# Experts and attention: statistics in two batches with powers on GpSimd, weight remainders spread over the steps, one-hot rows column by column

## The chip, the cores and the metric

The kernel runs on one core of one Trainium2 chip, as one launch. The metric is the device time in microseconds (us). The median of the three timed runs before the change is 2083.06 us.

## What is computed

`x` is (4, 1024, 256) in fp32, that is 4096 tokens of 256 numbers. Four layers follow one another; each normalises its input by rows and adds its result to `x`:

```python
x = x + attn_a(layernorm(x))     # a recurrent memory over chunks of 64 tokens
x = x + ffn(layernorm(x))        # 8 experts, 2 per token, and a shared one
x = x + attn_b(layernorm(x))     # softmax attention, 16 heads of 16
x = x + ffn(layernorm(x))

def layernorm(x):  return (x - mean(x)) / sqrt(var(x) + 1e-5)
def ffn(x):        # I = 352
    probs = softmax(x @ gate_w.T);  w, i = top_k(probs, 2);  w = w / w.sum()
    combine = sum(one_hot(i, 8) * w)
    out = sum_e combine[e] * ((silu(x @ w_gate[e]) * (x @ w_up[e])) @ w_down[e])
    return out + sigmoid(x @ shared_gate_w) * ((silu(x @ sw_gate) * (x @ sw_up)) @ sw_down)
```

Attention runs over four sequences of 1024 tokens.

## The kernel before

The residual X stays in on-chip memory as 32 tiles of 128 rows by 256. The kernel is a sequence of phases with a barrier between them: memory (`attn_a`), experts (`ffn_phase`, tag moe1), query/key/value projection (`qkv_phase`), scores, output projection, experts again (moe2). Within a phase each engine has its own instruction stream, written out by hand, and the streams meet at semaphores; so the order in each stream is the order of the work. Each phase that adds to X also leaves `stats` (bn_stats) of its rows for the next phase's normalisation.

**Opening of an expert phase.** VectorE (L404 to L415) aggregates the statistics of all 32 tiles into `mv` (L408, `var_done`), waits for `w_high`, subtracts the high part of the shared expert's weights (L412, one 128x1428 operation, `w_rest`), waits for `std_done` and takes the reciprocal of the root (L414). ScalarE (L308 to L314) loads the Sqrt table, copies the router's columns, casts the shared weights to their high part (L311), takes the root (L313) and loads the Silu table. Then VectorE normalises tile 0 (L431) and TensorE, which has waited, transposes it (L719).

**Precision.** Weights and rows are each split into a high part (fp32r) and a remainder; gate and up are three products (L794, L795, L799). The high parts of the 8 experts' weights are cast in 16 pieces of 128x704 by ScalarE (`weights_high`, L319) and the remainders subtracted by VectorE (`weights_rest`, L423), in place: `W_rest` lies where `W_gate_up` lay. The first 20 steps use the shared expert alone, so the experts' remainders are needed from step 20 on.

**Steps.** Step n handles one tile of 128 rows: transposition (L719), gate and up, silu (ScalarE, L341) times up (VectorE, `hidden`, L600), transposition of that (L809), down (L824), and the addition to X (`add_shared`, L604). `source_rest` (L427) subtracts the remainder of the transposed rows. The first four steps (LOOK = 4) are "looking" steps: beside its own tile each transposes 7 more (BESIDE = 7) and computes their router logits (`extra`, `extras`, L736), so that after step 3 all 32 tiles have logits. VectorE's own step n issues `hidden` for step n + 1 and `source_rest` for n + 2; in the looking steps it ends with `weights_rest`: 2, 4, 5 and 5 pieces. In step 4 `choose_first` copies the logits out of their bank (L459, `lg_ready`), for which down(4) waits; steps 4 to 7 choose the experts, count and compute positions.

**One-hot pieces.** In steps 8 to 15 (`one_hots(i)`, 8 columns each) VectorE compares broadcasts into `hot_j` (L552, 128x576) and `hot_p` (L554, 128x1024) and multiplies (L557, 128x576), all bf16, with drains between; ScalarE scales `hot_j` by the lane (`lanes`, L349). TensorE multiplies the pieces (`inverse`, L753) into a table of which token goes to which slot. After that come the routed blocks, fetched and sent by GpSimd's indirect DMAs (L269, L278).

**Attention.** `qkv_phase` opens as the experts do, without weights: Sqrt table, 8 memsets, 32 aggregations, root, reciprocal, then four tiles at a time (CT = 4) are normalised (`rows`, L1746), transposed (L1786) and projected (L1806). `out_projection_phase` opens with four copies by ScalarE (L2122) that TensorE transposes (L2148).

**GpSimd** builds constants at the start of an expert phase (L245 to L258), then waits for the slots. In the memory phase it takes one square root per chunk as a power (L1028).

## Time and profile before

| | us |
|---|---|
| median of three timed runs | 2083.06 |
| the three runs | 2081.0, 2083.06, 2090.43 |
| the profiled execution | 2093.06 |
| its span, first to last instruction | 2091.3 |

| engine | busy us | share of the span |
|---|---|---|
| TensorE (matmuls) | 1950.0 | 93% |
| VectorE | 1273.1 | 61% |
| ScalarE | 1136.9 | 54% |
| GpSimd | 424.3 | 20% |

The phases in the profiled execution, by the start of their first instructions: experts from 272.0 us, attention's projection from 733.7, output projection from about 1584.3, experts again from 1625.0. The mean granted TensorE clock is 0.965 of full.

How to read it: a line number is that of the kernel before. PE is TensorE's matmuls, PEld its weight loads, DVE is VectorE, ACT ScalarE, POOL GpSimd, SPq the queue that issues DMAs. A timeline row merges neighbouring instructions of one kind: its second number runs from the start of the first to the end of the last. In square brackets stands how long the engine was idle before the row and what released it. PEclk is the granted clock as a part of 2.4 GHz.

### The profile page before, as it was taken

To read this page: it belongs to the slowest core of one execution; us is meant where nothing else is said; L and a number is where in the kernel's file an instruction comes from. 1 tells how busy PE (TensorE), PEld (TensorE's weight loads), DVE (VectorE), ACT (ScalarE), POOL (GpSimd) and SP (SyncE) were. 2 spreads that over 40 slices of the span, in tenths; PEclk is the share of its full clock that TensorE was granted. 3 is DMA by queue.
4 is the path that set the end of the run, shared out by engine and by line. 5 is a ranking of instruction groups with operands and counts; after the bars stand their busy time and mean duration, and the time that the engine had idled before them with its cause. 6 is when DMAs were issued, how large, how long until landed. Compare 5 with 4: busy or idle time off the path is not lost. (4 is left out here: it accounts for less than half of the span.)

```text
span 2091.3 us, 52175 instructions
## 1 busy us (share of the span) xinstructions
PE 1950.0 (93%) x19334; PEld 1476.0 (71%) x19335; DVE 1273.1 (61%) x2596; ACT 1136.9 (54%) x2301; POOL 424.3 (20%) x495
## 2 busy tenths in 40 slices
PE   6899888999999879899999999999998889999997
PEld 6577677899999743355556555565546778999996
DVE  6455457622222857699999999999935585222226
ACT  2311153344444243389889899898995533444442
POOL 1021100255544132200000000000000002555542
PEclk9999969999999989999999999999999799999999
DMA  7000021122222456332111221111004211222226
GB/s 282 0 1 0 0 91 29 35 70 71 71 70 72 178 151 173 104 87 53 39 39 39 53 54 44 38 39 38 3 3 192 91 31 34 71 70 70 70 73 258
DMA packets 85433, 151.03 MB, mean 72 GB/s; under 512 B 35844, under 2 KB 67844, under 8 KB 78916
## 3 DMA queue, kind: packets, MB, share of 16 engines
q1 hardware_dynamic: 71620, 110.09, 17.3%
q0 software_dynamic: 13632, 38.41, 6.0%
q8 instruction: 129, 2.11, 0.4%
q14 instruction: 52, 0.43, 0.1%
HBM read 99.30 MB, written 48.76 MB: 71 GB/s over the span
## 5 line engine op out<-in xcount | busy, mean ns | idle before, releaser
L1932 ACT ACTIVATE att_scores_pt<-att_scores_psE 128x512 f32<-128x512 f32 x1024 | 598.1, 597 | 68.3 <-PE att_scores_psE L1535 26.0
L1550 DVE TENSOR_REDUCE att_mx<-att_scores_psS 128x1 f32<-128x1024 f32 x472 | 578.1, 1225 | 49.5 <-PE att_scores_psS L1535 18.1
L1535 PE MATMUL att_scores_psE<-att_qs,att_ks 99*32 99x512 bf16 x4096 | 438.0, 382 | 6.2 <-DVE att_scores_psO L1962 5.5
L2034 PE MATMUL att_scores_psO<-att_scores_pt,att_va 128*17 128x256 f32 x4096 | 330.5, 379 | 2.9 <-ACT att_scores_osb L1937 1.3
L824 PE MATMUL moe_ps<-W_down,work 128*128 (+1 forms) x1236 | 309.6, 387 | 13.9 <-DVEq L460 6.5
L1535 PE MATMUL att_scores_psS<-att_ks,att_qs 96*32 96x512 bf16 x3776 | 308.8, 380 | 0.1
L795 PE MATMUL moe_ps<-W_rest,moe_srcT_high 128*128 (+2 forms) x824 | 271.5, 330 | 0.0
L591 DVE SCALAR_TENSOR_TENSOR moe_pick<-work,moe_pick 128x2 f32 (+1 forms) x142 | 22.8, 161 | 407.9 <-PE moe_ps L799 407.9
L824 PEld LDWEIGHTS moe_ps<-W_down,work 128*128 128x128 f32 x1236 | 221.6, 192 | 42.8 <-issue 19.1
L1535 PEld LDWEIGHTS att_scores_psE<-att_qs,att_ks 99*32 99x32 bf16 x4096 | 136.8, 95 | 105.3 <-ACT att_scores_pt L1932 8.7
L2034 PEld LDWEIGHTS att_scores_psO<-att_scores_pt,att_va 128*17 128x17 f32 x4096 | 132.1, 98 | 102.4 <-issue 12.9
L794 PE MATMUL moe_ps<-moe_gate_up_high,moe_srcT_high 128*128 x568 | 196.5, 346 | 0.0
L269 POOL DMA_INDIRECT work<-normalised_rows,moe_slots_i x142 | 138.0, 972 | 287.3 <-DVE moe_slots_i L577 244.7
L278 POOL DMA_INDIRECT expert_rows<-work,moe_slots_i x142 | 140.2, 987 | 248.3 <-ACT work L356 236.7
L1535 PEld LDWEIGHTS att_scores_psS<-att_ks,att_qs 96*32 96x32 bf16 x3776 | 126.8, 98 | 77.3 <-issue 1.3
L337 ACT CAST moe_srcT_high<-moe_ps 128x256 fp32r<-128x256 f32 x206 | 76.6, 372 | 166.2 <-PE moe_ps L719 166.2
L795 PEld LDWEIGHTS moe_ps<-W_rest,moe_srcT_high 128*128 128x128 f32 x824 | 159.8, 194 | 0.0
L345 ACT COPY work<-moe_ps 128x384 f32<-128x384 f32 x206 | 97.8, 475 | 110.8 <-PE moe_ps L809 110.8
L356 ACT ACTIVATE work<-moe_ps,moe_y_weight 128x256 f32<-128x256 f32 x142 | 67.3, 474 | 154.6 <-PE moe_ps L824 154.6
L341 ACT ACTIVATE moe_hid<-moe_ps 128x352 f32<-128x352 f32 x206 | 95.4, 463 | 81.1 <-PE moe_ps L799 81.1
L799 PE MATMUL moe_ps<-moe_gate_up_high,moe_srcT_rest 128*128 x568 | 138.1, 324 | 0.0
L600 DVE TENSOR_TENSOR moe_hid<-moe_hid,moe_ps 128x352 f32<-128x352 f32 x206 | 106.6, 518 | 41.4 <-PE moe_ps L799 38.4
(286 smaller groups left out, 2739.3 us busy)
## 6 DMA issues: line engine op xcount, KB each, us to landing
work<-expert_rows SPq DMA_DIRECT2D x16, 1024.0 KB, 6.6
W_gate_up<-in_gate_up_dram SPq DMA_DIRECT2D x2, 6346.0 KB, 21.9
query_key_parts<-att_qkv_parts SPq DMA_DIRECT2D x64, 192.0 KB, 2.8
normalised_rows<-work SPq DMA_DIRECT2D x64, 128.0 KB, 1.8
work<-normalised_rows SPq DMA_DIRECT2D x56, 128.0 KB, 2.2
att_qs<-query_key_parts SPq DMA_DIRECT2D x16, 384.0 KB, 4.3
att_ks<-query_key_parts SPq DMA_DIRECT2D x16, 384.0 KB, 4.4
W_down<-in_down_a_dram SPq DMA_DIRECT2D x2, 2304.0 KB, 27.3
```

The source lines that it names most:

```text
L269: nc.gpsimd.indirect_dma_start(out=src[u][:, :], out_offset=None, in_=xn_d, in_offset=bass.IndirectOffsetOnAxis(ap=slots_i[:, j, 0:1].bitc ...
L278: nc.gpsimd.indirect_dma_start(out=ys, out_offset=bass.IndirectOffsetOnAxis(ap=slots_i[:, j, 1:2].bitcast(U32), axis=0), in_=yb[j % 2][:, ...
L345: nc.scalar.copy(hidT[u][:, :, :].rearrange("p k t -> p (k t)"), psH[:, 0:IP]).then_inc(hidT_ready, 1)
L600: nc.vector.tensor_tensor(hid[u][:, 0:I], hid[u][:, 0:I], psU[u][:, 0:I], ALU.mult).then_inc(hid_ready, 1)
L794: nc.tensor.matmul(psum, srcT_high[u][:, k, :], high(k), start=(k == 0), stop=False)
L795: nc.tensor.matmul(psum, srcT_high[u][:, k, :], rest(k), start=False, stop=False)
L799: last = nc.tensor.matmul(psum, srcT_rest[u][:, k, :], high(k), start=False, stop=(k == KD - 1))
L824: last = nc.tensor.matmul(psD[:, 0:D], hidT[u][:, k, :], W["down"][:, k, e, :], start=(k == 0), stop=(k == KI - 1))
L1535: last = nc.tensor.matmul(out[j:j + 32, :], stationary[:, j:j + 32], moving, start=True, stop=True, tile_position=(0, j), skip_group_check ...
L1550: return nc.vector.tensor_reduce(a.mx[g % 2][:, v:v + 1], bank[:, :, :].rearrange("p h k -> p (h k)"), AX.X, ALU.max)
L1932: nc.scalar.activation(pt[s % 2][:, r, :], psE[use % E_BANKS][:, :], ACT.Exp, scale=HD ** -0.5).then_inc(p_ready, 1)
L2034: last = nc.tensor.matmul(psO[32 * r:32 * r + VC, cols], va[g][:, kt, r * VC:(r + 1) * VC], pt[s % 2][:, r, cols], start=(kt == 0 and part ...
```

## The change

In the expert phases:

- The statistics are aggregated in two batches, the first 11 tiles (FIRST = LOOK + BESIDE) and the other 21. VectorE adds eps into `spread`, and GpSimd raises it to the power -0.5 into `rstd`. Root, reciprocal and both table loads go.
- ScalarE copies router columns and casts the shared weights in two halves; VectorE subtracts them in two halves (`shared_rest`), one ahead of the wait for the first powers, one between extra(1) and source_rest(0).
- The second batch of statistics, and the wait for its powers, stand behind the extras of step 0 and ahead of those of step 1.
- GpSimd casts the first four of the experts' 16 weight pieces, ScalarE the other twelve, in looking steps 0 to 2. The remainders are subtracted in steps 0, 1, 2 (4, 4 and 8 pieces), in two portions around `hidden`, instead of 2, 4, 5, 5 at the ends of steps 0 to 3.
- The one-hot rows are written by 3 x 8 tensor-scalar operations per piece, of 128, 72 and 72 columns, each against a pointer to a column of `pos_p` or `pos_j` (now fp32). `hot_j`, `tile1` and ScalarE's `lanes` go.

In `qkv_phase` the same split of the statistics (4 and 28 tiles) with powers on GpSimd; the memsets of `vt` move behind the second batch. In `out_projection_phase` ScalarE loads the Silu table first.

The diff, cut to its core:

```diff
@@ -183,6 +181,11 @@
+        def weights_high(nc, copy, i):
...
+            e, k = divmod(i, KD)
+            return copy(H[:, k, e * GU:(e + 1) * GU], W["gate_up"][:, k, e * GU:(e + 1) * GU])
@@ -242,6 +245,13 @@
         def _(pool):
+            nc.gpsimd.memset(minus_half[:, :], -0.5).then_inc(half_set, 1)
+            pool.wait_ge(half_set, 1)
+            for i, some in enumerate((slice(0, FIRST), slice(FIRST, NT))):
+                pool.wait_ge(var_done, i + 1)
+                nc.gpsimd.tensor_tensor(rstd[:, some], spread[:, some], minus_half[:, some], ALU.pow).then_inc(rstd_ready, 1)
+            for i in range(KD * E // LOOK):
+                weights_high(nc, nc.gpsimd.tensor_copy, i).then_inc(w_high, 1)
@@ -305,18 +314,10 @@
         def _(act):
-            nc.scalar.preload_act_table(ACT.Sqrt)
...
-            nc.scalar.copy(router[:, :, :], W["gate_up"][:, :, (E + 1) * GU:])
-            nc.scalar.copy(W["shared_high"][:, :, :], W["gate_up"][:, :, E * GU:]).then_inc(w_high, 1)
-            act.wait_ge(var_done, 1)
-            nc.scalar.activation(rstd[:, :], mv[:, :, 1], ACT.Sqrt, bias=eps[:, :]).then_inc(std_done, 1)
-            nc.scalar.preload_act_table(ACT.Silu)
...
-            def weights_high(i):
...
-                e, k = divmod(i, KD)
-                nc.scalar.copy(H[:, k, e * GU:(e + 1) * GU], W["gate_up"][:, k, e * GU:(e + 1) * GU]).then_inc(w_high, 1)
+            for k in range(KD):
+                nc.scalar.copy(router[:, k, :], W["gate_up"][:, k, (E + 1) * GU:])
+                nc.scalar.copy(W["shared_high"][:, k, :], W["gate_up"][:, k, E * GU:]).then_inc(shared_high, 1)
             def extra_out(x):
@@ -369,15 +366,13 @@
-                if 0 <= here - LOOK - 6 < CH // PIECE:
-                    lanes(here - LOOK - 6)
...
-                        if i < 2 + KD * E // LOOK:
-                            weights_high(n * (KD * E // LOOK) + i - 2)
+                        if n + 1 < LOOK and i < 2 + KD * E // LOOK:
+                            weights_high(nc, nc.scalar.copy, (n + 1) * (KD * E // LOOK) + i - 2).then_inc(a_high, 1)
@@ -401,25 +396,27 @@
         def _(dve):
-            nc.vector.memset(eps[:, :], EPS)
-            for u in range(2):
-                nc.vector.memset(hid[u][:, I:IP], 0.0)
-            for t in range(NT):
-                nc.vector.bn_aggr(mv[:, t, :], stats[:, t, :])
-            dve.drain().then_inc(var_done, 1)
-            dve.wait_ge(w_high, 1)
-            raw = W["gate_up"][:, :, E * GU:]
-            nc.vector.tensor_tensor(W["rest"][:, :, E * GU:], raw, W["shared_high"][:, :, :], ALU.subtract).then_inc(w_rest, 1)
-            dve.wait_ge(std_done, 1)
-            nc.vector.reciprocal(rstd[:, :], rstd[:, :])
-            dve.drain().then_inc(rstd_ready, 1)
+            def spreads(some):
+                for t in range(some.start, some.stop):
+                    nc.vector.bn_aggr(mv[:, t, :], stats[:, t, :])
+                dve.drain()
+                nc.vector.tensor_scalar(spread[:, some], mv[:, some, 1], EPS, None, ALU.add).then_inc(var_done, 1)
...
+            def shared_rest(k):
+                dve.wait_ge(shared_high, k + 1)
+                nc.vector.tensor_tensor(W["rest"][:, k, E * GU:], W["gate_up"][:, k, E * GU:], W["shared_high"][:, k, :],
+                                        ALU.subtract).then_inc(w_rest, 1)
             def weights_rest(some):
+                by_pool = KD * E // LOOK
...
-                    dve.wait_ge(w_high, i + 2)
+                    if i < by_pool:
+                        dve.wait_ge(w_high, i + 1)
+                    else:
+                        dve.wait_ge(a_high, i - by_pool + 1)
...
             def source_rest(n, u):
@@ -543,18 +540,14 @@
             def one_hots(i):
-                c = slice(i * PIECE, (i + 1) * PIECE)
-                over = lambda v, n: v[:, c, None].to_broadcast([P, PIECE, n])
-                if i:
-                    dve.wait_ge(lane_done, i)
                 if i >= 2:
                     dve.wait_ge(inv_done, i - 1)
-                nc.vector.tensor_tensor(hot_j[:, :, :], iota_j[:, None, :].to_broadcast([P, PIECE, NBT]),
-                                        over(pos_j, NBT), ALU.is_equal).then_inc(hot_ready, 1)
-                nc.vector.tensor_tensor(hot_p[i % 2][:, :, :], iota_p[:, None, :].to_broadcast([P, PIECE, P]),
-                                        over(pos_p, P), ALU.is_equal)
-                dve.drain()
-                nc.vector.tensor_tensor(hot_id[i % 2][:, :, 0, :], hot_j[:, :, :], over(tile1, NBT), ALU.mult)
+                for c in range(PIECE):
+                    at = i * PIECE + c
+                    at_p, at_j = pos_p[:, at:at + 1], pos_j[:, at:at + 1]
+                    nc.vector.tensor_scalar(hot_p[i % 2][:, c, :], iota_p[:, :], at_p, None, ALU.is_equal)
+                    nc.vector.tensor_scalar(hot_id[i % 2][:, c, 0, :], iota_j[:, :], at_j, float(at + 1), ALU.is_equal, ALU.mult)
+                    nc.vector.tensor_scalar(hot_id[i % 2][:, c, 1, :], iota_j[:, :], at_j, lane[:, :], ALU.is_equal, ALU.mult)
                 dve.drain().then_inc(inv_ready, 1)
             def slots():
@@ -633,10 +626,14 @@
+                if k == "shared" and n < len(RESTS):
+                    weights_rest(RESTS[n][0])
...
+                if k == "shared" and n < len(RESTS):
+                    weights_rest(RESTS[n][1])
@@ -646,15 +643,23 @@
-                    weights_rest(((0, 1), (2, 3, 4, 5), (6, 7, 8, 9, 10), (11, 12, 13, 14, 15))[n])
-
+
+            RESTS = (((0, 1), (2, 3)), ((4, 5), (6, 7)), (range(8, 14), (14, 15)))
+            spreads(slice(0, FIRST))
+            shared_rest(0)
+            dve.wait_ge(rstd_ready, 1)
             normalise(src[0], 0).then_inc(src_ready, 1)
             extra(0)
...
+            shared_rest(1)
             source_rest(0, 0)
             normalise(src[1], 1).then_inc(src_ready, 1)
...
+            for u in range(2):
+                nc.vector.memset(hid[u][:, I:IP], 0.0)
+            spreads(slice(FIRST, NT))
+            dve.wait_ge(rstd_ready, 2)
             extras(1, range(4))
             hidden(0, 0)
@@ -890,13 +894,13 @@
-            pe.wait_ge(w_rest, 1)
+            pe.wait_ge(w_rest, KD)
...
-                    pe.wait_ge(w_rest, 1 + KD * E)
+                    pe.wait_ge(w_rest, KD + KD * E)
@@ -1729,16 +1735,11 @@
         def _(dve):
-            nc.vector.memset(eps[:, :], EPS)
-            for u in range(2):
-                for j in range(CT):
-                    nc.vector.memset(vt[u][j][:, :, HD:VC], 1.0)
-            for t in range(NT):
-                nc.vector.bn_aggr(mv[:, t, :], stats[:, t, :])
-            dve.drain().then_inc(var_done, 1)
-            dve.wait_ge(std_done, 1)
-            nc.vector.reciprocal(rstd[:, :], rstd[:, :])
-            dve.drain()
+            def spreads(some):
+                for t in range(some.start, some.stop):
+                    nc.vector.bn_aggr(mv[:, t, :], stats[:, t, :])
+                dve.drain()
+                nc.vector.tensor_scalar(spread[:, some], mv[:, some, 1], EPS, None, ALU.add).then_inc(var_done, 1)
             def rows(c):
@@ -1751,8 +1752,15 @@
+            spreads(slice(0, CT))
+            dve.wait_ge(rstd_ready, 1)
             rows(0)
+            spreads(slice(CT, NT))
+            for u in range(2):
+                for j in range(CT):
+                    nc.vector.memset(vt[u][j][:, :, HD:VC], 1.0)
             dve.wait_ge(*weights_loaded)
+            dve.wait_ge(rstd_ready, 2)
             for c in range(NCH):
                 u = c % 2
@@ -2114,6 +2122,8 @@
         def _(act):
+            nc.scalar.preload_act_table(ACT.Silu)
...
             def rows_out(t, u):
```

## Rows read from the trace of the kernel before

**Rows 1.** Page, part 1: engine, busy us, share of the span, instructions.

```profile
PE 1950.0 (93%) x19334; PEld 1476.0 (71%) x19335; DVE 1273.1 (61%) x2596; ACT 1136.9 (54%) x2301; POOL 424.3 (20%) x495
```

**Rows 2.** Timeline, first expert opening: start, us, engine, line, out<-in, [idle before <-releaser].

```profile
272.02 1.28 ACT L308 ACT_TABLE_LOAD   x1 [19.72 <-PEq L47]
...
272.17 2.19 DVE L408 BATCH_NORM_AGGREGATE moe_mv<-stats 128x2 f32<-128x6 f32 x32
...
273.43 1.38 ACT L311 CAST W_shared_high<-W_gate_up 128x1428 fp32r<-128x1428 f32 x1
...
274.84 1.65 DVE L412 TENSOR_TENSOR W_rest<-W_gate_up,W_shared_high 128x1428 fp32r<-128x1428 f32 x1 [0.47 <-ACT W_shared_high L311]
...
276.87 1.06 DVE L431 TENSOR_SCALAR work<-X,moe_mv,moe_rstd 128x256 f32<-128x256 f32 x3
...
277.34 1.12 PE L719 MATMUL moe_ps<-ident,work 128*128 128x128 f32 x4 [7.55 <-DVE work L431]
...
278.81 2.67 DVE L431 TENSOR_SCALAR work<-X,moe_mv,moe_rstd 128x256 f32<-128x256 f32 x8
```

**Rows 3.** Timeline, attention opening.

```profile
737.04 1.38 DVE L1746 TENSOR_SCALAR att_qkv_xn<-X,att_qkv_mv,att_qkv_rstd 128x256 f32<-128x256 f32 x4
...
738.47 1.97 PE L1786 MATMUL att_qkv_ps<-ident,att_qkv_xn 128*128 128x128 f32 x8 [8.45 <-DVE att_qkv_xn L1746]
```

**Rows 4.** Timeline, end of the four looking steps, first expert phase.

```profile
317.90 0.48 DVE L604 SCALAR_TENSOR_TENSOR X<-moe_ps,moe_sg,X 128x256 f32<-128x256 f32 x1 [3.52 <-PE moe_ps L824]
...
318.86 4.09 DVE L423 TENSOR_TENSOR W_rest<-W_gate_up,moe_gate_up_high 128x704 fp32r<-128x704 f32 x5
...
323.73 0.55 PE L809 MATMUL moe_ps<-ident,moe_hid 128*128 128x128 f32 x3 [1.13 <-DVE moe_hid L600]
...
329.68 2.00 PE L824 MATMUL moe_ps<-W_down,work 128*128 128x256 f32 x6 [3.24 <-DVEq L460]
...
335.12 0.52 DVE L600 TENSOR_TENSOR moe_hid<-moe_hid,moe_ps 128x352 f32<-128x352 f32 x1 [1.71 <-PE moe_ps L799]
```

**Rows 5.** Windows: stretch, length, busy us per engine (instructions), PEclk, DMA share, GB/s.

```profile
289.00:293.00 4.00, 4.00 (x21) 4.00 (x21) 2.04 (x6) 2.02 (x6) 0.00 (x0) 0.50 0.30 102
330.00:334.00 4.00, 4.00 (x16) 3.64 (x15) 2.83 (x8) 0.48 (x1) 0.00 (x0) 0.58 0.00 0
1654.00:1658.00 4.00, 4.00 (x15) 3.55 (x15) 0.68 (x2) 1.27 (x3) 0.00 (x0) 0.50 0.28 95
```

**Rows 6.** Timeline of VectorE, first one-hot pieces of the second expert phase.

```profile
1710.17 0.75 DVE L552 TENSOR_TENSOR work<-moe_iota_j,moe_pos_j 128x576 bf16<-128x576 bf16 x1
...
1713.01 0.48 DVE L604 SCALAR_TENSOR_TENSOR X<-moe_ps,moe_sg,X 128x256 f32<-128x256 f32 x1
...
1714.17 0.75 DVE L552 TENSOR_TENSOR work<-moe_iota_j,moe_pos_j 128x576 bf16<-128x576 bf16 x1
```

**Rows 7.** Timeline of VectorE, two settled one-hot steps, first phase.

```profile
368.36 0.48 DVE L604 SCALAR_TENSOR_TENSOR X<-moe_ps,moe_sg,X 128x256 f32<-128x256 f32 x1
...
372.69 0.48 DVE L604 SCALAR_TENSOR_TENSOR X<-moe_ps,moe_sg,X 128x256 f32<-128x256 f32 x1
```

**Rows 8.** Groups by shape on GpSimd: line, op, tiles, shapes, count, busy us, mean ns.

```profile
L1028 POOL TENSOR_TENSOR mem_root<-mem_n,mem_halfpow 128x4 f32<-128x4 f32 x16 | 16.2, 1011 | 91.5 <-DVE mem_n L1265 91.5
...
L1560 POOL TENSOR_TENSOR att_mxr<-att_mx 128x32 f32<-128x32 f32 x16 | 4.0, 248 | 2.3
```

**Rows 9.** Groups by shape on VectorE: tensor-scalars with pointers, with one column, with immediates.

```profile
L431 DVE TENSOR_SCALAR work<-X,moe_mv,moe_rstd 128x256 f32<-128x256 f32 x64 | 24.2, 411 | 19.2 <-PE moe_ps L719 18.1 <-issue 0.6
...
L448 DVE TENSOR_SCALAR moe_sg<-moe_half_gate 128x1 f32<-128x1 f32 x8 | 1.2, 149 | 0.0
...
L1163 DVE TENSOR_SCALAR work<-W 128x512 f32<-128x512 f32 x1 | 0.4, 425 | 0.0
```

**Rows 10.** Timeline, opening of the output projection.

```profile
1584.69 1.32 ACT L2122 COPY out_o<-work 128x256 f32<-128x256 f32 x4 [6.67 <-PEq L2276]
...
1585.15 1.12 PE L2148 MATMUL out_psT<-ident,out_o 128*128 128x128 f32 x4 [6.42 <-ACT out_o L2122]
```

30 lines of the change are left out of this document (13 added, 17 removed).

## Prediction

> **What bounds the kernel now.** I read the page first: TensorE is busy 93% of a span of 2091.3 us and VectorE 61% [rows 1], so work saved on VectorE or ScalarE counts only where TensorE stands still for it. Then I read the stretches that the change touches, in order of time: the opening of an expert phase, the opening of the attention phase, the end of the four looking steps, the steps with one-hot pieces, and the opening of the output projection. There are two expert phases; the rows are of the first except where I say otherwise, and the second shows the same pattern.
>
> In the opening [rows 2] the reader should follow who waits for whom. VectorE aggregates all 32 tiles (2.19 us), ScalarE splits the shared weights (1.38) and only then takes the root; VectorE puts the subtraction of the shared weights (1.65) in front of the reciprocal, so the first normalisation starts at 276.87 and TensorE's first transpose at 277.34, after 7.55 us of nothing. The attention phase opens alike [rows 3]: rows at 737.04, transposes at 738.47, after 8.45 us of nothing. At the end of the looking steps [rows 4] VectorE runs two blocks of five remainders, 4.09 us each. Behind the first comes hidden(4), for which TensorE has waited 1.13 us when it transposes it at 323.73; behind the second, the logits are copied late and TensorE waits 3.24 us for `lg_ready` (DVEq L460). In the 4 us behind that wait the granted clock averages 0.58 of full, near the 1.2 GHz level, which the next matmuls pay for [rows 5].
>
> In the one-hot steps VectorE needs 2.84 us for a piece (1710.17 to 1713.01) and 1.16 us for the rest of the step when it is not held up (1713.01 to 1714.17), 4.00 together [rows 6]. Yet the settled step takes 4.33 us (368.36 to 372.69) [rows 7]: TensorE sets it, its window has no idle time. VectorE's slack is 0.33 us a step, so a piece may cost 3.17 us before it moves the end. That one number decides much of this forecast.
>
> **The change part by part.**
>
> *Opening of the experts.* Eleven aggregations instead of 32: at (2.19 - 0.15)/31 = 0.066 us each, they end near 272.9. A small addition (0.15, as L448 [rows 9]) gives the spread at about 273.2. Removed from the path are table load, root, reciprocal and the whole shared subtraction; in their place stands a power on GpSimd. The trace has one, 128x4 at 1.01 us; a 128x32 subtraction there takes 0.25 [rows 8], so some 0.8 us of the 1.01 are the power itself. For 128x11 the bounds are 1.0 (all of it fixed) and 0.2 + 11 x 0.2 = 2.4 (all by element). I take 1.8, between the two, since one row can't part them. First normalisation then at 275.2, bounds 274.4 to 275.9, against 276.87: 1.7 us earlier. The half subtraction shared_rest(0) (about 0.89, the L423 price) is hidden under the power; shared_rest(1) now stands ahead of source_rest(0), for which TensorE waits: -0.4. Net 1.3, bounds 0.6 to 2.1.
>
> *The second batch* of statistics (21 tiles, 1.4 us) and its power (1.0 to 4.4) are a new wait on VectorE. Queued behind it are extras 7 to 13 and hidden(0), for which TensorE would wait at about 290, some 13 us after the first normalisation, because the clock is at half there [rows 5]. By adding up, VectorE resumes 7.3 to 10.9 us after that normalisation and owes 3 us; the cover is thin only at the slow end. Cost 0; without the cold clock, and with the slow power, it would be 2 us. GpSimd's four weight splits come behind it in its queue and are first read a step later; its iotas are needed much later still.
>
> *Remainders spread.* The total stays 16 per phase, 0.82 each. Steps 0 and 1 get four instead of two and four, step 2 gets eight instead of five, step 3 none. In step 0 they delay add_shared and source_rest(2) by 0.2 to 0.4 us. In step 2 VectorE stood idle for 3.52 us [rows 4], which hides them. In step 3 hidden(4) follows its matmuls instead of five remainders: the 1.13 us wait goes. The next thing late is again `lg_ready`: down(4) could start near 325.2, and the logits' copy, behind hidden(5) and source_rest(6), ends near 326.6. So 1.4 us of the 3.24 stay. From there I lay out the steps at the full-clock durations: hidden(6), at 335.12 before [rows 4], comes at about 330.5. That is 4.6 us, of which 1.1 and 1.8 are waits and the rest is the cold stretch. If the clock falls all the same, 2.6. Less 0.3 for step 0: 4.3.
>
> *One-hot pieces.* Three wide broadcast operations, two drains and a ScalarE operation become 24 small tensor-scalars with pointer operands. An L431 tensor-scalar, with two pointers at 4 bytes, takes 0.411 for 256 columns and 0.149 where there is one (L448): one column a cycle [rows 9]. Eight back to back take 2.67 (a start every 0.32), so 0.09 of each overlaps [rows 2]. At that rate 128 columns cost 0.19 and 72 cost 0.135: 8 x (0.19 + 2 x 0.135) = 3.7 us a piece, above 3.17. L1163, an immediate at 4 bytes, does 512 columns in 0.425: two a cycle [rows 9]. At that rate it is 8 x (0.128 + 2 x 0.098) = 2.6 us, below 3.17, and TensorE sets the step. L431 is nearest in having pointers. The new operands, however, are 2 bytes wide, half the traffic of either row, and no row has that form. I take the faster end, with a chance not far from even. Gain there: 0.5 us a phase, in the first pieces, which VectorE still sets. Cost at the slow end: 1.16 + 3.7 + 0.1 = 4.9 a step, 0.6 x 16 = 9 us, and the 1.0 us of gain is lost too.
>
> The Trainium skill (VectorE: DVE Perf Modes, "The perf-mode tier table") gives tensor_scalar four elements a cycle at bf16 and two at fp32, in SBUF. L1163 agrees; L431 does not, at half the fp32 rate. As an estimate, the page's four a cycle would make a piece about 2.0 us, and since TensorE sets the step, the forecast would stay.
>
> *Attention opening.* Four aggregations, the spread, and the one power whose price a row gives exactly (1.01): rows(0) at about 735.5 instead of 737.04 [rows 3]. The weights' DMAs don't come into it, TensorE waits for the rows. Gain 1.5. The second power (28 columns, 1.0 to 5.8) holds VectorE until at latest 745, near its next need: cost 0, at worst 1.7.
>
> *Output projection.* The Silu table (1.28, L308 in [rows 2]) now loads ahead of the first copy at 1584.69, for which TensorE already waits 6.42 us [rows 10]. It is fully on the path: +1.3. In the second expert phase nothing else is bought by it than is counted above.
>
> **Sum.** First experts 1.3 + 4.3 + 0.5 = 6.1; attention 1.5; second experts 6.1; projection -1.3: 12.4 us. Part of the openings' gain is time at half clock, and if the clock's rise keeps its place it is worth half: I take off 1.4, leaving 11. The profiled execution took 2093.06 with a span of 2091.3; it would become 2082. Against the median of the three timed runs, 2083.06, that is **2072 us**. The runs themselves spread over 9 us (2081.0 to 2090.43), and TensorE's cold stretch at the second opening lasts to about 1658 in this execution, longer than at the first (about 293) [rows 5]. So the clock alone makes or hides some 5 us.
>
> **The rivals.**
>
> *A: pointers run at one column a cycle.* For it: all the L431 rows. Against: their width. 11 - 10 = 1 us of gain: 2082 us. Chance 0.30.
>
> *B: small instructions do not overlap (the slower side).* If each of the 24 shows its whole duration (0.28 for 128, 0.22 for 72 columns), a piece takes 5.8 us and a step 7.0, 2.6 x 16 = 42 us more: 2114 us. The kernel turns slower from a mean start-to-start of about 0.16 us on. Against it: eight L431 rows overlap. Chance 0.07.
>
> *C: the clock rises earlier.* TensorE's idle time before each opening shrinks, and if the look steps then run at 2.4 GHz, the cold 28 us of the second phase give back up to 13: 2060 us. Against: the first phase starts cold anyway. Chance 0.10.
>
> *D: the part at the end of looking brings little*, because another operation holds VectorE there, or the clock falls again; 2 to 4 us less per phase: 2078 us. Chance 0.13.
>
> **How the numbers follow.** The forecast has 0.40. Low end 2063: the fast powers (1.6 us over both phases) and several us of luck with the clock. High end 2086: A with the slow powers and less luck. I leave B and the far part of C outside. About 0.5% (10.4 us) is what a measurement can tell from no change: faster means under 2072.6, slower over 2093.5. The forecast lies at that edge, so some 0.6 of its chance, nearly all of C and little of the rest counts as faster: 0.42. Slower is B and a little of A: 0.09. The rest, 0.49, is within.
>
> **What would show it.** In the profile of the changed kernel: the first transpose at about 275.7 and no idle time on TensorE for hidden(4); a wait of 1 to 2 us for the logits' copy instead of 3.24, with no drop of the clock behind it; one-hot tensor-scalars at most 0.13 us apart and a step of 4.3 us; the attention's first rows less than 2 us after that phase starts; a table load ahead of the projection's first copy. Wrong would be: a piece above 3.2 us, TensorE waiting on the one-hots, a GpSimd power over 2.4 us for eleven columns, or TensorE waiting for hidden(0) behind the second power.

## The result and the profile after

The changed kernel takes 2094.56 us (median of 20 runs, 2089.31 to 2107.28), the kernel before 2079.61 (20 runs, 2070.71 to 2090.43). The ratio is 1.0076, 95% interval 1.0058 to 1.0094: some 15 us slower, where 2072 with a range of 2063 to 2086 was forecast. The profiled execution of after took 2093.50, near its median. That of before took 2093.06, some 13 us above its median, so the two spans must not be set against each other: the comparison below goes stage by stage.

The page of after, first line and part 1, answers to [rows 1]. VectorE has 338 instructions more and 24 us more of busy time.

```profile
span 2091.8 us, 52460 instructions
...
PE 1943.5 (93%) x19334; PEld 1464.5 (70%) x19335; DVE 1296.8 (62%) x2934; ACT 1118.5 (53%) x2274; POOL 449.4 (21%) x510
```

**One-hot pieces.** Timeline of VectorE in after, one piece and the add_shared row that ends it (start, us, engine, line, out<-in).

```profile
346.35 0.25 DVE L548 TENSOR_SCALAR work<-moe_iota_p,moe_pos_p 128x128 bf16<-128x128 bf16 x1
346.51 0.24 DVE L549 TENSOR_SCALAR work<-moe_iota_j,moe_pos_j 128x72 bf16<-128x72 bf16 x1
346.66 0.30 DVE L550 TENSOR_SCALAR work<-moe_iota_j,moe_pos_j,moe_lane 128x72 bf16<-128x72 bf16 x1
346.86 0.25 DVE L548 TENSOR_SCALAR work<-moe_iota_p,moe_pos_p 128x128 bf16<-128x128 bf16 x1
...
350.71 0.48 DVE L597 SCALAR_TENSOR_TENSOR X<-moe_ps,moe_sg,X 128x256 f32<-128x256 f32 x1
...
356.24 0.48 DVE L597 SCALAR_TENSOR_TENSOR X<-moe_ps,moe_sg,X 128x256 f32<-128x256 f32 x1
...
361.76 0.48 DVE L597 SCALAR_TENSOR_TENSOR X<-moe_ps,moe_sg,X 128x256 f32<-128x256 f32 x1
```

A column of the piece costs 0.51 to 0.52 us (346.35 to 346.86), the piece 4.36 (346.35 to 350.71) against 2.84 [rows 6]. The settled step is 5.52 us (356.24 to 361.76) against 4.33 [rows 7]: exactly 4.36 plus the 1.16 of the rest, so VectorE sets it now. TensorE waits for the end of the one-hots (timeline of TensorE, [idle before <-releaser]):

```profile
356.20 0.67 PE L757 MATMUL moe_ps<-work 128*128 128x144 bf16 x8 [0.84 <-DVEq L551]
```

**Openings.** Timeline of VectorE and GpSimd in after, first experts' opening; it answers to [rows 2].

```profile
272.16 0.84 DVE L401 BATCH_NORM_AGGREGATE moe_mv<-stats 128x2 f32<-128x6 f32 x11 [0.97 <-PEq L47]
...
276.06 1.06 DVE L428 TENSOR_SCALAR work<-X,moe_mv,moe_rstd 128x256 f32<-128x256 f32 x3 [2.00 <-POOL moe_rstd L252]
...
281.75 0.18 DVE L403 TENSOR_SCALAR moe_spread<-moe_mv 128x21 f32<-128x21 f32 x1
285.73 3.16 DVE L428 TENSOR_SCALAR work<-X,moe_mv,moe_rstd 128x256 f32<-128x256 f32 x4 [3.80 <-POOL moe_rstd L252]
288.81 0.51 DVE L593 TENSOR_TENSOR moe_hid<-moe_hid,moe_ps 128x352 f32<-128x352 f32 x1
```

The powers, as groups by shape on GpSimd in after (count | busy us, mean ns):

```profile
L252 POOL TENSOR_TENSOR moe_rstd<-moe_spread,moe_minus_half 128x21 f32<-128x21 f32 x2 | 7.4, 3693 | 11.9 <-DVE moe_spread L403 11.9
...
L188 POOL CAST moe_gate_up_high<-W_gate_up 128x704 fp32r<-128x704 f32 x8 | 6.2, 816 | 0.0
L252 POOL TENSOR_TENSOR moe_rstd<-moe_spread,moe_minus_half 128x11 f32<-128x11 f32 x2 | 5.3, 2636 | 2.3 <-DVE moe_spread L403 2.3
L1687 POOL TENSOR_TENSOR att_qkv_rstd<-att_qkv_spread,att_qkv_minus_half 128x28 f32<-128x28 f32 x1 | 4.8, 4795 | 3.6 <-DVE att_qkv_spread L1742 3.6
```

The reader should see two things behind the second power. VectorE stands 3.80 us for it. Then four normalisations take 3.16 us, which is 0.79 each where eight took 2.67 before [rows 2]: GpSimd's casts of 0.82 us run at that time. Together hidden(0) starts 18.9 us after TensorE's last work before the opening, where it was 15.9.

**End of the looking steps, attention, projection**, timeline of TensorE in after, for [rows 4], [rows 3] and [rows 10]:

```profile
326.07 1.53 PE L828 MATMUL moe_ps<-W_down,work 128*128 128x256 f32 x6 [1.37 <-DVEq L457]
...
738.29 1.97 PE L1794 MATMUL att_qkv_ps<-ident,att_qkv_xn 128*128 128x128 f32 x8 [6.98 <-DVE att_qkv_xn L1747]
...
1587.18 1.12 PE L2158 MATMUL out_psT<-ident,out_o 128*128 128x128 f32 x4 [8.03 <-ACT out_o L2132]
```

**By stages.** Worked out from the start times of VectorE's hidden rows (L600 before, L593 after) and from TensorE's timeline; E is the end of TensorE's last work before an opening, h(n) the start of hidden(n). "Before, again" is the trace of the experiment of that name. Each cell has the first and the second expert phase, in us.

```
                              E to h(3)        h(3) to h(9)     h(9) to h(18)
before                        44.07  49.53     37.22  37.17     39.50  38.44
before, again                 44.71  43.00     35.63  35.60     38.44  38.42
after                         44.85  44.15     30.84  30.72     48.29  48.69
old one-hots                  49.53  44.14     30.83  31.12     38.44  38.43
old one-hots, no spread       48.41  42.97     35.00  35.24     38.44  38.42
before, new one-hots          44.63  45.09     35.58  37.88     48.23  48.20
experts' root                 41.22  40.44     30.85  31.08     38.44  38.41
early statistics              40.06  39.70     30.83  31.11     38.43  38.43
```

Each part of the change has its main column. The one-hots act in the third, and lose 9.8 to 10.3 us a phase against 38.44. The remainders act in the second: 4.8 us less than "before, again", and 4.1 to 4.2 less with all else equal (rows 4 and 5). But 1.1 to 1.2 of that is hidden(3) itself coming later on VectorE, behind the remainders of steps 0 to 2: the first column is 49.53 against 48.41 and 44.14 against 42.97, with the clock on the same course in both. From E to h(9) the spread gains 3.0 us a phase. The opening acts in the first column, where the clock spreads the values more than the change does.

### The profile page after: what moved, and what is told of

It is laid out like the page before. It is cut to its first block and busy times, and to the rows that moved or that the text cites. A ratio compares the mean times of both kernels' runs of the same rounds, so it can differ in the third digit from the quotient of the medians.

```text
span 2091.8 us, 52460 instructions
## 1 busy us (share of the span) xinstructions
PE 1943.5 (93%) x19334; PEld 1464.5 (70%) x19335; DVE 1296.8 (62%) x2934; ACT 1118.5 (53%) x2274; POOL 449.4 (21%) x510
## 5 line engine op out<-in xcount | busy, mean ns | idle before, releaser
L2042 PE MATMUL att_scores_psO<-att_scores_pt,att_va 128*17 128x256 f32 x4096 | 330.5, 379 | 2.9 <-ACT att_scores_osb L1945 1.3
L1562 POOL TENSOR_TENSOR att_mx<-att_mx,att_zeros 128x32 bf16<-128x32 f32 x16 | 4.2, 260 | 616.5 <-DVE att_mx L1554 616.5
```

The source lines that it names most:

```text
L2042: last = nc.tensor.matmul(psO[32 * r:32 * r + VC, cols], va[g][:, kt, r * VC:(r + 1) * VC], pt[s % 2][:, r, cols], start=(kt == 0 and part ...
```

## The experiments

**1. The one-hots undone, with all the rest kept.** In one_hots the comparisons go back to wide operations:

```diff
-                    nc.vector.tensor_scalar(hot_p[i % 2][:, c, :], iota_p[:, :], at_p, None, ALU.is_equal)
...
+                nc.vector.tensor_tensor(hot_p[i % 2][:, :, :], iota_p[:, None, :].to_broadcast([P, PIECE, P]),
+                                        over(pos_p, P), ALU.is_equal)
...
+                nc.vector.tensor_tensor(hot_id[i % 2][:, :, 0, :], hot_j[:, :, :], over(tile1, NBT), ALU.mult)
```

> The changed kernel with the one-hot pieces undone: three wide broadcast operations on VectorE and the lane product on ScalarE, as before; all other parts of the change stay. Theory (the piece is the cost): in the changed kernel's trace a piece takes 4.36 us and the settled step 5.52, against 2.84 and 4.33; over hidden(8) to hidden(17) that adds 8.8 us per phase, 17.5 in both, of which 1.6 at a time can be swallowed by a wait for a gather. Undone it gives back 14 to 18 us of the 2094.6: 2077 to 2081, with a settled step of 4.33 and the phase's earlier gain of 5.2 us at hidden(8) kept to its end. First rival (the rest of the change gains what its traces show, some 10 us, and the pieces cost all of the difference to the result, 25): 2069 to 2071. Second rival (the pieces only fill time in which TensorE would wait for the first gathered rows, and powers or the table load cost the time): 2090 or more.

Measured: 0.9967 of before (0.9950 to 0.9984), 2079.07 beside 2087.04 on that chip. The settled step is 4.33 again. Against the 1.0076 of after that is 1.09%, 22.7 us of 2080, give or take 5. The traces show 20.1 of them: after's two values in the third column less twice 38.43. The comparisons are the cost, as the theory says, and the second rival (2090 or more) falls. The theory's size was set too low: the first rival's 25 us for the pieces lies inside 22.7 give or take 5, and its 10 us for the rest of the change at the far edge of what was measured (0.33%, 7 us, give or take 3.5). The reason is that 8.8 us a phase had been read from hidden(8) to hidden(17) in the first phase against the profiled execution of before, in which that stretch took 1.1 us more than in the other trace of before (41.97 against 40.90).

**2. The new one-hots alone**, put into the kernel before; the edit is the reverse of experiment 1.

> The kernel before with the one-hot pieces alone changed into 24 comparisons per column. Theory: 14 to 18 us slower than before, 2094 to 2098 against a median of 2079.6, with a settled step of 5.5 us and TensorE waiting for the inverse's one-hots in each. First rival: 25 us slower, 2105. Second rival: within 3 us of before, because the steps end on something else.

Measured: 1.0082 (1.0051 to 1.0113), 17 us slower than before, give or take 6. So the comparisons alone make all of the loss, within the intervals.

**3. Old one-hots and the remainders as before** (2, 4, 5 and 5 at the steps' ends).

```diff
-                if k == "shared" and n < len(RESTS):
-                    weights_rest(RESTS[n][0])
...
+                    weights_rest(((0, 1), (2, 3, 4, 5), (6, 7, 8, 9, 10), (11, 12, 13, 14, 15))[n])
```

> The same as the kernel with the old one-hot pieces, and the remainders too as before (2, 4, 5 and 5 at the ends of the four looking steps). Theory: the spread is worth what the traces show at hidden(6), 5.2 us less the opening's 0.7, so 4.5 us a phase and 9 in both, less what the gather's wait takes: 7 to 9 us slower than with the spread. Rival: the clock makes most of it (behind the 3.24 us wait the granted clock fell to 0.58 in the profiled execution of before, but need not fall in every execution): 2 to 5 us slower. Another rival: nothing, because the first gathered rows set the end of this stretch.

Measured: 1.0011 (0.9992 to 1.0030), so the spread is worth 0.44%, 9.2 us, give or take 5. The stages say 3.0 us a phase from E to h(9), 6.0 in both. That is what TensorE's two waits lose. Its timeline without the spread, where the second wait is 1.37 us with it:

```profile
321.83 0.55 PE L825 MATMUL moe_ps<-ident,moe_hid 128*128 128x128 f32 x3 [1.12 <-DVE moe_hid L607]
327.77 1.53 PE L840 MATMUL moe_ps<-W_down,work 128*128 128x256 f32 x6 [3.24 <-DVEq L467]
```

What is left of the change here (statistics in two batches, powers, four casts on GpSimd, the table load) comes out at 0.11% the other way: no gain that can be measured.

**4. The kernel before, a second trace.**

> The kernel before, unchanged, for a second trace. Its first profiled execution (2093.06) lies 13 us above the median of 20 runs (2079.6). Theory: TensorE's stretch at 1.2 GHz at the second experts' opening, which lasted to about 1658 there, 28 us after the opening, is of another length in each execution; where it ends after some 15 us, as in the first phase, the run is 8 to 13 us shorter. Rival: the excess lies elsewhere (transfers, the attention), and the second opening looks as it did.

Measured: 2080.24. Its second phase reaches h(3) 43.00 us after E instead of 49.53, its clock being at half for 17 us (13.7 and 3.4) instead of 31, and behind the wait for the logits the clock does not fall this time: h(3) to h(9) is 1.6 us shorter in both phases. Another 5.1 us lie ahead of the first opening, in a stretch where no two kernels of this study differ (TensorE's last work there ends between 263.5 and 270.2 in all thirteen traces). So the theory holds for half of the excess of 12.8 us between the two spans (6.5, under the 8 to 13 that it gave). The rest lies in other places: the 5.1 us ahead of the first opening, for which no cause is known, and 1.6 us twice behind the logits; together these are more than the excess, so other stages give some of it back.

**5. Half the width, twice the number.**

```diff
-                    nc.vector.tensor_scalar(hot_p[i % 2][:, c, :], iota_p[:, :], at_p, None, ALU.is_equal)
+                    for h in (slice(0, P // 2), slice(P // 2, P)):
+                        nc.vector.tensor_scalar(hot_p[i % 2][:, c, h], iota_p[:, h], at_p, None, ALU.is_equal)
```

and the same for the other two.

> The changed kernel with each of the 24 comparisons of a piece cut into two of half the width (64 or 36 columns), 48 instructions for the same output. Theory: such an instruction costs a fixed time, and its columns nearly nothing (starts 0.16 apart for 128 columns, 0.15 for 72, 0.21 for 72 with two pointers): a piece takes 7.8 to 8.2 us instead of 4.36, the settled step 9.1, and the run is 16 x 3.5 = 56 us longer than the changed kernel, 2145 to 2155. Rival: the columns cost the time, halves cost half: the piece stays below 5 us and the run below 2105.

Measured: 2158.96 in one run, 4 us above the theory's range; the settled step is 9.12, the theory's 9.1. Groups by shape on VectorE there, from 360 to 400 us:

```profile
L552 DVE TENSOR_SCALAR work<-moe_iota_j,moe_pos_j,moe_lane 128x36 bf16<-128x36 bf16 x72 | 20.5, 285 | 0.0
L551 DVE TENSOR_SCALAR work<-moe_iota_j,moe_pos_j 128x36 bf16<-128x36 bf16 x71 | 15.9, 224 | 0.0
L549 DVE TENSOR_SCALAR work<-moe_iota_p,moe_pos_p 128x64 bf16<-128x64 bf16 x70 | 13.1, 229 | 0.0
```

Half the columns take 285, 224 and 229 ns there (288, 227 and 233 over the whole trace), where all took 302, 241 and 252. Nearly all of the time belongs to the instruction, not to its columns.

**6. The operation by itself.** Behind each old piece, 21 tensor-scalars into a tile that nobody reads:

```diff
+                for n, values, first, last in ((P, iota_p, 5.0, None), (P, iota_p, lane[:, :], None), (NBT, iota_j, 5.0, 3.0),
+                                               (NBT, iota_j, lane[:, :], 3.0), (NBT, iota_j, lane[:, :], lane[:, :])):
+                    for at in range(0, 4 * P, P):
+                        nc.vector.tensor_scalar(spare[:, at:at + n], values[:, :], first, last, ALU.is_equal,
+                                                *((ALU.mult,) if last is not None else ()))
+                    dve.drain()
+                nc.vector.tensor_scalar(spare[:, :], hot_p[i % 2][:, 0:4, :].rearrange("p c q -> p (c q)"), lane[:, :], None, ALU.is_equal)
```

> A measurement of one operation by itself: the kernel with the old one-hot pieces, and behind each piece 21 tensor-scalars into a tile that nobody reads, in groups of four with a drain behind each group: 128 columns against an immediate, 128 against a pointer, 72 with two immediates, 72 with pointer and immediate, 72 with two pointers, and one of 512 columns against a pointer. All at 2 bytes. Theory (each instruction costs a fixed time, the pointers add some and columns little): the pointer forms start 0.15 to 0.16 apart, the form with two pointers 0.21, the immediates not much less (0.12 to 0.16), and 512 columns take about 0.33 us, that is 0.25 for 128 plus 384 columns at the 0.2 ns which 128 against 72 columns shows. Rival (pointers make the columns slow): 512 columns take 0.65 us or more, at one column a cycle, and the immediates start 0.08 apart or less. The run's time only carries the added work, about 16 x 4 us.

The one run took 2145.40 us, with the added work. Timeline of VectorE, then its groups by shape in the first expert phase:

```profile
363.89 0.50 DVE L569 TENSOR_SCALAR moe_spare<-moe_iota_p 128x128 bf16<-128x128 bf16 x4
364.47 0.74 DVE L569 TENSOR_SCALAR moe_spare<-moe_iota_p,moe_lane 128x128 bf16<-128x128 bf16 x4
365.29 0.45 DVE L569 TENSOR_SCALAR moe_spare<-moe_iota_j 128x72 bf16<-128x72 bf16 x4
```

```profile
L569 DVE TENSOR_SCALAR moe_spare<-moe_iota_p,moe_lane 128x128 bf16<-128x128 bf16 x32 | 6.0, 251 | 0.6
...
L569 DVE TENSOR_SCALAR moe_spare<-moe_iota_p 128x128 bf16<-128x128 bf16 x32 | 4.0, 190 | 1.0
L569 DVE TENSOR_SCALAR moe_spare<-moe_iota_j 128x72 bf16<-128x72 bf16 x32 | 3.6, 178 | 0.6
L572 DVE TENSOR_SCALAR moe_spare<-work,moe_lane 128x512 bf16<-128x512 bf16 x8 | 2.8, 353 | 0.6
```

A pointer adds 61 ns to the duration at 128 columns (251 less 190), 63 at 72 (241 in after less 178), a second pointer another 61 (302 less 241). Starts lie (0.50 - 0.19)/3 = 0.10 us apart with immediates and (0.74 - 0.25)/3 = 0.16 with a pointer. At 72 columns they lie 0.09, 0.15 and 0.21 us apart with none, one and two pointers, each form in a group of its own. Four times the columns, 512 against 128, add 102 ns, 0.27 ns each. The rival (slow columns) falls. The theory's guess that immediates cost not much less falls with it at 0.10: as an estimate from these distances, the 24 comparisons would take some 2.3 us with immediates, and with pointers they take 8 x (0.16 + 0.15 + 0.21) = 4.2. The pointers here are of 4 bytes; no run has them at 2.

**7. Two comparisons a column**, the lane entries made by ScalarE:

```diff
-                    nc.vector.tensor_scalar(hot_id[i % 2][:, c, 1, :], iota_j[:, :], at_j, lane[:, :], ALU.is_equal, ALU.mult)
...
+                    act.wait_ge(hot_ready, at + 1)
+                    last = nc.scalar.activation(hot_id[i % 2][:, c, 1, :], hot_id[i % 2][:, c, 0, :], ACT.Copy, scale=ratio[:, at:at + 1])
```

> The changed kernel with two comparisons per column instead of three: the 16 with one pointer stay on VectorE, and ScalarE makes the lane entries out of the tile entries, eight small operations a piece with a factor lane/(tile + 1) from a table made once. Theory (each comparison costs its start-to-start time, and only what passes 3.17 us a piece moves the end): a piece takes 8 x (0.16 + 0.15) = 2.5 us, VectorE's share of the step is 3.65, and the settled step falls back from 5.52 to TensorE's 4.33; the run comes to the time with the old one-hot pieces, 0.995 to 0.998 of before against 1.0076. Rival: ScalarE's eight operations, which can't start before the comparisons and take some 0.2 us each, become what TensorE waits for: step 4.6 to 5.2, run 1.000 to 1.005. Another rival: comparisons with pointers cost more when ScalarE reads beside them, step above 5: 1.005 or more.

Measured: 1.0045 (1.0021 to 1.0069), a settled step of 4.96. VectorE has time to spare; ScalarE is what TensorE waits for (timelines of VectorE, ScalarE and TensorE):

```profile
358.95 0.52 DVE L606 TENSOR_TENSOR moe_hid<-moe_hid,moe_ps 128x352 f32<-128x352 f32 x1 [0.99 <-ACT moe_hid L344]
...
356.42 2.07 ACT L354 ACTIVATE work<-work,moe_ratio 128x72 bf16<-128x72 bf16 x8
358.40 0.44 ACT L344 ACTIVATE moe_hid<-moe_ps 128x352 f32<-128x352 f32 x1
...
358.63 0.66 PE L771 MATMUL moe_ps<-work 128*128 128x144 bf16 x8 [0.46 <-ACT work L354]
```

The first rival holds: the piece of 2.5 us no longer bounds the step, but ScalarE's eight small operations, 2.07 us, hold back the hidden row queued behind them. The fixed price of small operations had only been moved to another engine. That a cheap piece brings back 4.33 is shown by the wide form alone.

**8. The statistics of the other 21 tiles ahead of the first wait** (on top of the old one-hots):

```diff
             spreads(slice(0, FIRST))
             shared_rest(0)
+            spreads(slice(FIRST, NT))
             dve.wait_ge(rstd_ready, 1)
...
-            spreads(slice(FIRST, NT))
             dve.wait_ge(rstd_ready, 2)
```

> The kernel with the old one-hot pieces, the remainders spread and the powers kept, but VectorE aggregates the other 21 tiles straight after the first shared remainder, while it waits for the first power, instead of behind the eleven normalisations, so that GpSimd runs the second power right behind the first. Theory: in the trace with the old one-hot pieces TensorE, at full clock from 278 on, waited 0.43 and 2.31 us around 283 to 286 because VectorE stood 3.8 us for the second power, and then ran at half clock to 302, which costs 8.5 us of clock; with the power 4 us earlier the waits go and, where the clock had risen before, the second fall too. 3 to 8 us faster than with the old one-hot pieces alone (0.9967 of before), so 0.993 to 0.995 of before. Rival: the clock falls there whatever the waits are, and in the other executions TensorE is slow enough that it never waited: no difference, 0.9967.

Measured: 0.9929 (0.9905 to 0.9953), 0.38% below experiment 1, give or take 0.29: 8 us, give or take 6. First the trace of experiment 1, TensorE and VectorE, then windows (start:end, length, busy us of PE, PEld, DVE, ACT and POOL, PEclk, DMA share, GB/s):

```profile
282.53 3.16 DVE L438 TENSOR_SCALAR work<-X,moe_mv,moe_rstd 128x256 f32<-128x256 f32 x4 [3.81 <-POOL moe_rstd L255]
...
283.42 0.44 PE L738 MATMUL moe_ps<-ident,work 128*128 128x128 f32 x2 [0.43 <-DVE work L438]
286.17 0.90 PE L828 MATMUL moe_ps<-ident,moe_hid 128*128 128x128 f32 x3 [2.31 <-DVE moe_hid L607]
```

```profile
279.00:283.00 4.00, 3.91 (x31) 3.35 (x30) 0.47 (x1) 3.79 (x8) 4.00 (x2) 1.00 0.21 69
284.00:300.00 16.00, 13.83 (x59) 13.52 (x60) 10.25 (x22) 6.29 (x15) 3.38 (x12) 0.52 0.37 124
```

The first window ends where the waits begin, the second takes in the longer wait. The clock had risen before 279; TensorE then stood 0.43 and 2.31 us for rows held up by the second power, and worked the next 16 us at 0.52 of full, near 1.2 GHz. With the statistics early both are gone (timeline of VectorE and window of that kernel):

```profile
269.98 1.06 DVE L438 TENSOR_SCALAR work<-X,moe_mv,moe_rstd 128x256 f32<-128x256 f32 x3 [0.34 <-POOL moe_rstd L255]
```

```profile
276.00:300.00 24.00, 23.55 (x179) 21.75 (x178) 19.63 (x43) 18.11 (x45) 2.55 (x12) 1.00 0.48 152
```

VectorE's wait of 2.00 us for the first power is filled with the aggregations, and the column E to h(3) falls from 49.53 to 40.06. In the second phase of experiment 1 the clock took another course and the same edit gains 4.4. The two together are more than the runs' 8 us, because this trace is the fastest of its six runs (2062.94, median 2068.22).

One trace could show the fall by chance; the others bear it out. In six openings with the second power late the clock had risen 11 to 12 us after E (experiments 1 and 3, first phase; 7, both; 5 and 6, second phase), and in all six it fell again 18.0 to 18.5 us after E, for 10 to 17 us. In six with early statistics or the old root it had risen 11 to 13 us after E (8 and 11, both phases; 9 and 10, first phase), and in none did it fall again in the looking steps. A short fall of 3.4 us from 19.3 us on stands in four second phases, one of them of the kernel before, which has no second power; the wait does not explain that one.

**9. The table load moved** from the projection's head to the experts' opening, and **10.** with the statistics also ahead of the shared remainder (GpSimd now also waits for the weights ahead of its casts):

```diff
+            nc.scalar.preload_act_table(ACT.Silu)
             act.wait_ge(weights_loaded[0], weights_loaded[1])
```

```diff
             spreads(slice(0, FIRST))
-            shared_rest(0)
             spreads(slice(FIRST, NT))
+            shared_rest(0)
```

> The same as with the early statistics, and the Silu table is loaded at the head of the experts' opening on ScalarE instead of at the head of the output projection. Theory: the load stands fully ahead of the projection's first copy (TensorE waits 8.0 us there instead of 6.3) and is hidden in the experts' opening under VectorE's statistics and the first power: 1.6 us faster, once. Rival: it delays the shared weights' copies by 1.3 us in both phases, and with them the first matrix products, so it brings nothing or costs 1.

> The kernel with the early statistics and the table load in the experts' opening, with one more change of order: VectorE aggregates all its tiles (first 11, then 21) before the first shared remainder. Theory: in the trace with the table load there VectorE waited 1.08 us for the shared weights' copy with the 21 aggregations queued behind, and its first normalisation came 0.75 us late; with the aggregations ahead the wait is filled, TensorE's idle time at the opening is 6.64 us again instead of 7.39, and at the projection it stays 6.3 instead of 8.0. Together 0.990 to 0.994 of before, that is the early statistics' 0.993 less 1.6 us. Rival: the difference between 0.9929 and 0.9958 was the table load in another way (a lower clock at the opening, 11.9 us lost in the second phase of that trace): 0.995 or more.

Measured: 0.9958 (0.9936 to 0.9981) and 0.9913 (0.9884 to 0.9942). In 9 VectorE waited 1.08 us for the shared weights' copy, with the statistics queued behind, and TensorE's idle time at the opening was 7.39 us instead of 6.64: no gain, and the mechanism of its rival. The rival's size, at most 1 us, is not what sets 9 and 8 apart: they differ by 0.29%, give or take 0.33, and in the trace of 9 the clock of the second opening rose only 28.5 us after E (11.0 in 8), and h(3) comes 7.9 us later. In 10 the idle time is 6.21, its theory holds and its rival (0.995 or more) falls; at the projection TensorE waits less than the 7.94 of experiment 8:

```profile
1570.49 1.12 PE L2173 MATMUL out_psT<-ident,out_o 128*128 128x128 f32 x4 [6.71 <-ACT out_o L2147]
```

The table load on the projection's path is worth 1.2 us by this. The kernel of 10, median 2065.31, beats the kernel before by 0.87% and the changed one by 1.6%; its lead of 0.16% over the one of 8 lies within the intervals.

**11. Old statistics, root and reciprocal in the experts' opening**, powers in the attention alone. The table load ahead of the projection goes too, and GpSimd's casts start behind the first extras.

```diff
-                nc.gpsimd.tensor_tensor(rstd[:, some], spread[:, some], minus_half[:, some], ALU.pow).then_inc(rstd_ready, 1)
...
+            nc.scalar.activation(rstd[:, :], mv[:, :, 1], ACT.Sqrt, bias=eps[:, :]).then_inc(rstd_ready, 1)
```

> The kernel with the old one-hot pieces, the remainders spread, and in the experts' opening the statistics, the table load, the root and the reciprocal of the kernel before (no power); GpSimd's four casts stay, but start behind the first extras. The attention keeps its powers, the output projection has no table load. Theory: the first transposes come 0.9 us later in each phase, but no second power holds VectorE, so no wait for hidden(0), and the projection starts 1.6 us earlier: 2 to 6 us faster than with the old one-hot pieces alone, 0.994 to 0.996 of before. Rival: the powers' 0.9 us a phase counts more than the second power costs: 1 us slower, 0.997.

Measured: 0.9939 (0.9916 to 0.9962), 0.28% below experiment 1, give or take 0.28, and no different from experiment 8. The first transposes do come later (7.58 us of idle time against 6.64, and 7.58 against 6.29 in the second phase), and hidden(0) 4.3 and 4.7 us sooner. So in the experts' opening the powers, even in their best order (8 and 10), have not been shown to beat the old root.

## Why the prediction was wrong

**One-hot pieces: the step that failed.** It put a piece between 2.6 and 3.7 us and took the fast end; it took 4.36, outside both. The forecast had the threshold right: VectorE's slack was 0.33 us, a piece may cost 3.17, and what passes that lengthens every step (4.36 - 3.17 = 1.19, and 5.52 - 4.33 = 1.19). It had the price wrong, because it read the price as one per column. The L431 row, 0.411 for 256 columns, was divided by its columns, after taking off the 0.149 of L448 as the fixed part [rows 9]. But L448 has immediates. With two pointers the fixed part is some 0.28 us (0.302 less 72 x 0.27 ns), which leaves 0.13 for the 256 columns of L431, half a nanosecond each: by this estimate, which carries a price measured at 2 bytes over to 4, the row that was taken for a slow column rate was a fast one behind two pointers. No run has that form with immediates. Both ends of the range and rival A were built on that reading. The start-to-start distance, which rival B named as the point of decision at 0.16 us, was the right quantity: it came out at 0.16, 0.15 and 0.21, mean 0.173. B's mechanism (no overlap at all) was not what happened, its threshold was. Eight L431 rows back to back, a start every 0.32 [rows 2], were the nearest row; taking off the columns at either rate of the forecast leaves 0.06 to 0.18 for the rest, so 24 of them cost 1.4 to 4.3 us before any column of theirs is counted. That was the range that the rows allowed, and its upper part lay above 3.17.

The Trainium skill (VectorE: DVE Perf Modes, "The TRN2 errata — SBUF-src ops pay a fixed extra latency per instruction") says that each instruction pays a fixed cost, so that many small tiles pay it once each, and advises tiles of 512 elements or more; it speaks against this edit and was not weighed. Its formula, with that page's clock and its tier of four columns a cycle, gives as an estimate 0.09 us for 128 columns and 0.08 for 72, which the distances between starts with immediates, 0.10 and 0.09, nearly bear out, and those with a pointer, 0.16 and 0.15, do not. The four elements a cycle of the section that the prediction did cite agree with 0.27 ns a column, and decided nothing.

**The sum.** Forecast 1.0 us of gain for the one-hots, measured a loss of 20 in the traces and 17 to 23 in the runs. That term alone turns the forecast of 11 us of gain into a loss of about 10 (21 us between the gain and the loss). By the runs, the spread gained 9 us (forecast 8.6) and the rest lost 2, give or take 4 (forecast a gain of about 1.4, with 1.4 taken off for the clock): 23 - 9 + 2 makes the loss of some 15.

**Remainders spread: right mechanism, size partly luck.** Forecast 4.3 us a phase, measured 3.0 by the traces with all else equal; the runs' 9.2 us in both, give or take 5, fit either. TensorE's wait for hidden(4) is gone, 1.37 us of the 3.24 are left for the logits (forecast 1.4), and hidden(6) came at 329.91 (forecast 330.5). The part put down to the cold stretch, 1.7 of the 4.6, was not steady: in the second trace of before, and without the spread in experiment 3, the clock stayed up behind the same 3.24 us, and what remained to gain were the waits, 1.12 + 1.87.

**Openings: right mechanism, sizes off, and a cover that failed.** The power over eleven columns took 2.64 us (taken 1.8, upper bound 2.4, and over 2.4 was named as a sign of being wrong), so the first normalisation gained 0.8 instead of 1.7, and the first matrix products 0.6 instead of 1.3. The second power, 3.69, lay inside its bounds. "Cost 0, or 2 us without the cold clock" was mis-sized at its far end. In after's first phase TensorE stood at half clock and hid the wait. Where the clock had risen (experiment 1's trace, shown under 8), TensorE waited 2.7 us, and behind that came 16 us at about half clock, some 8 us of lost time, which is more than the wait. The casts were named as standing behind the power in GpSimd's queue, but not that VectorE's normalisations more than double beside them. The Trainium skill (Perfetto Trace Analysis, "Optimizing Scalar/DVE Operations") says that GpSimd and VectorE share a port to SBUF; the 0.79 us rows agree, in the experts' opening with the old root too (two in 1.28 us beside the same casts), and no run here shows that it is the port.

**Attention and projection: right.** 8.45 us of idle time became 6.98 (forecast 1.5 less). For the second power, 4.80 us, VectorE stood 4.76 us, and TensorE did not wait behind it: "cost 0" was right. The table load costs 1.2 to 1.6 us (forecast 1.3).

**The base.** The profiled execution of before was known to stand 10 us above the median of three, and it stood 13 above that of twenty. Taking the difference over unchanged was sound, and the forecast's 5 us for the clock were too few: one and the same stretch, E to h(3), took between 43.0 and 49.5 us in four phases of the same kernel.

## What to carry to other kernels

Price a small VectorE instruction by its start-to-start distance in a row of the same form, pointers included, before any rate per column: here 0.10 us with immediates, 0.16 with one pointer, 0.21 with two, nearly the same from 36 to 128 columns of 2 bytes. Splitting a wide operation pays only if the number of pieces times that distance is below what the wide one takes, and moving the pieces to another engine moves the same kind of cost there. When a wait is split in two, put the second batch's preparation ahead of the first wait, and look for who stands behind the second at full clock, not at the clock of one trace.

## What was not expected of the hardware

- Each pointer operand of 4 bytes costs a VectorE tensor-scalar about 61 ns, in duration and in start distance (0.09 or 0.10, 0.15 or 0.16, 0.21 us with none, one and two); 384 more columns at 2 bytes cost 102 ns.
- A GpSimd power takes 1.05, 2.64, 3.69 and 4.80 us for 4, 11, 21 and 28 columns of 128 partitions: 0.23 us a column to eleven, then 0.11 and 0.16.
- Two waits of 2.7 us in all on TensorE at full clock were followed by some 16 us at 0.52 of it, and in six openings of six such a fall came behind the late second power, in none of six without it. At the first opening of an expert phase in twelve traces (all but that of experiment 6) the clock rose for the first time 11 to 14 us after TensorE's last work before it (seven traces) or 23 to 25 us after (five, with the old opening and the new); in that of experiment 6 it was 28. What chooses between them was not settled.
